# Gated cross-attention block on one core: layer 0's key, value and context preparation on f16 parts, placed in the middle of a step

## What is computed

```python
# layer 0, differential attention: 32 score heads of 4, 16 value heads of 8
k = ctx @ Wk.T ; v = ctx @ Wv.T          # [32, 1500, 128] each
a1 = softmax(q1 @ k1.T / 2) @ v ; a2 = softmax(q2 @ k2.T / 2) @ v
attn = a1 - lam * a2                      # then RMS norm per head, Wp, bp
# layer 1, masked attention: 16 heads of 8, bias on q, k and v
k = ctx @ Wk.T + bk ; v = ctx @ Wv.T + bv
attn = softmax(where(mask, -inf, q @ k.T / sqrt(8))) @ v
x = x + tanh(g) * attention ; x = x + tanh(g) * experts
```

## Time and profile before

| | |
|---|---|
| median of 3 executions | 2541.89 us |
| the profiled execution | 2538.51 us |
| its span | 2536.7 us |
| PE / DVE / ACT / POOL busy | 93% / 66% / 58% / 42% |
| mean granted TensorE clock | 0.952 |

### The profile page before, as it was taken

How to read it: one execution, slowest core, us unless ns; L and a number is a source line. 1 busy time by engine, 2 the same in 40 slices (tenths; PEclk the granted TensorE clock), 3 DMA queues, 4 the chain that set the end, 5 groups by cost and what they waited for, 6 DMA issues and landing times. The chain is left out here.

```text
span 2536.7 us, 64926 instructions
## 1 busy us (share of the span) xinstructions
PE 2371.0 (93%) x26296; PEld 1320.2 (52%) x26296; DVE 1679.8 (66%) x3732; ACT 1471.6 (58%) x2101; POOL 1057.8 (42%) x1150
## 2 busy tenths in 40 slices
PE   4799999999999999999996976999999999999798
PEld 3244444444444444444444763566655666666576
DVE  2587777777777777777782553666666666666444
ACT  2156666666666666666675432566656666666422
POOL 4213323333333333332323347456655565663232
PEclk8589999999999999999997996899999999999799
DMA  3533434534434345343321006567665766753100
GB/s 101 104 72 76 96 95 74 112 78 91 103 78 100 91 78 109 77 96 96 74 43 49 22 28 141 107 127 135 131 121 119 123 133 126 135 130 51 51 1 14
DMA packets 157410, 227.67 MB, mean 90 GB/s; under 512 B 46052, under 2 KB 106596, under 8 KB 156612
## 3 DMA queue, kind: packets, MB, share of 16 engines
q1 hardware_dynamic: 157124, 223.67, 42.4%
HBM read 146.77 MB, written 76.48 MB: 88 GB/s over the span
## 5 line engine op out<-in xcount | busy, mean ns | idle before, releaser
L943 ACT ACTIVATE probs<-score_ps 125x896 f32<-125x896 f32 x1152 | 1011.4, 916 | 159.5 <-PE score_ps L850 158.6
L1001 DVE TENSOR_REDUCE max_part<-max_ps 112x1 f32<-112x500 f32 x1022 | 654.6, 670 | 177.0 <-PE spare_ps L829 87.6
L866 PE MATMUL acc_ps<-probs,vext 125*32 125x224 f32 (+1 forms) x12288 | 675.2, 315 | 3.4 <-issue 2.5
L829 PE MATMUL max_ps<-kstack,qstack 48*112 48x500 f16 x1533 | 522.1, 403 | 6.7 <-DVE max_part L1001 3.4
L1001 DVE TENSOR_REDUCE max_part<-spare_ps 112x1 f32<-112x500 f32 x514 | 344.2, 670 | 148.1 <-PE max_ps L829 147.1
L998 DVE CUSTOM_DVE_ANT_0 kstack<-max_ps,kstack 112x500 f32<-112x500 f32 x511 | 335.2, 675 | 160.2 <-PE max_ps L829 87.8
L720 POOL CAST khl<-kstack 128x500 f16<-128x500 f32 x192 | 115.0, 599 | 700.2 <-ACT kstack L926 510.2
L866 PEld LDWEIGHTS acc_ps<-probs,vext 125*32 125x32 f32 x12288 | 258.1, 108 | 262.2 <-issue 248.7
L850 PE MATMUL score_ps<-qstack,kstack 50*125 50x224 f16 (+1 forms) x6144 | 387.7, 243 | 3.3 <-ACT probs L943 1.9
L850 PEld LDWEIGHTS score_ps<-qstack,kstack 50*125 50x125 f16 x6144 | 304.5, 134 | 136.7 <-issue 95.1
L829 PE MATMUL spare_ps<-kstack,qstack 48*112 48x500 f16 x771 | 310.8, 403 | 7.0 <-DVE max_part L1001 1.9
(11 more groups left out here) (184 smaller groups left out, 2613.3 us busy)
## 6 DMA issues: line engine op xcount, KB each, us to landing
kstack<-k_parts SPq DMA_DIRECT2D x384, 187.5 KB, 6.6
k_parts<-khl SPq DMA_DIRECT2D x128, 375.0 KB, 5.5
ctx_f<-in_ctx SPq DMA_DIRECT2D x32, 750.0 KB
context_parts<-ctx_f SPq DMA_DIRECT2D x32, 750.0 KB, 4.7
ctx_f<-context_parts SPq DMA_DIRECT2D x32, 750.0 KB, 4.3
mask_in<-in_mask SPq DMA_DIRECT2D x128, 82.0 KB
qrows<-q_parts SPq DMA_DIRECT2D x384, 7.0 KB, 7.4
qstack<-max_rows SPq DMA_DIRECT2D x384, 0.9 KB
```

The source lines that it names most:

```text
L829: nc.tensor.matmul(room(("P", n, p))[0:PIECE, 0:TK], qstack[n % SLOTS][rows, c, PIECE * i:PIECE * (i + 1)], kstack[n % SLOTS][rows, c, TK ...
L866: last = nc.tensor.matmul(acc_ps[32 * j:32 * j + 32, TT * S * i:TT * S * (i + 1)].rearrange("p (s c) -> p s c", s=S), vext[n % SLOTS][:, t ...
L943: nc.scalar.activation(probs[t % 2][:, 896 * h:896 * h + 896].rearrange("k (b c) -> k b c", b=2), score_ps[(t * H + h) % 2][0:KT, :, 0:448 ...
L1001: nc.vector.reduce_max(best, scores, AX.X).then_inc(s_red, 1)
```

## The change

Both weights of both layers are scaled by 64 and split once, in the set-up, into an f16 high part and an f16 rest (`w_parts`). The context is split the same way. A projection is then three f16 matmuls into one accumulator (high by high, rest by high, high by rest). In layer 0, ACT copies the turned context as f32 into `context_f`, GpSimd makes the two parts from it in the loop (`split_context`), and DVE does so for the first three entries; there are now two buffers of parts. DRAM holds the parts, of the same size as before, and layer 1 reads them.

The side numbers of `where` get new meanings: 1 is between the two halves of the weighing, ahead of the second search, and 2 is behind the weighing. Layer 0's users are reordered, one for each step, on side 1 (A on side 2). Layer 1's stay behind the weighing; M moves there from its place behind the first search.

```diff
+                    for w in range(2):
+                        weight = small[f"W{'kv'[w]}T{i}"][:, :]
+                        high, low = w_parts[:, i, w, 0, :], w_parts[:, i, w, 1, :]
+                        link(nc.vector.tensor_scalar(weight, weight, QK_UP, None, ALU.mult))
...
+                        link(nc.vector.tensor_copy(high, weight))
+                        link(nc.vector.tensor_tensor(low, weight, high, ALU.subtract))
...
     if L is L0:
-        where = {("V", 0): (0, 1), ("F", 0): (1, 1), ("F", 1): (2, 1), ("V", 1): (3, 1), ("T", 0): (4, 1), ("V", 2): (5, 1),
-                 ("K", 0): (6, 1), ("M", 0): (7, 0), ("T", 1): (7, 1), ("K", 1): (8, 1), ("T", 2): (9, 1), ("K", 2): (10, 1),
-                 ("A", 0): (11, 1)}
-        keyed = [("T", 0), ("K", 0), ("T", 1), ("K", 1), ("T", 2), ("K", 2)]
+        where = {("T", 0): (0, 1), ("F", 0): (1, 1), ("T", 1): (2, 1), ("F", 1): (3, 1), ("T", 2): (4, 1), ("K", 0): (5, 1),
+                 ("V", 0): (6, 1), ("M", 0): (7, 1), ("K", 1): (8, 1), ("V", 1): (9, 1), ("K", 2): (10, 1), ("V", 2): (11, 1),
+                 ("A", 0): (11, 2)}
+        keyed = [(kind, i) for kind in "TK" for i in range(NTHIRD)]
...
             def store_context(n):
-                sp.wait_ge(s_ctxT, NTHIRD * (n + 1))
+                sp.wait_ge(s_cp, low_part(n, LAST_THIRD))
...
+            def split_context(n, i):
+                k = slice(TK * i, TK * i + TK)
+                pool.wait_ge(s_ctxT, NTHIRD * n + i + 1)
...
+                nc.gpsimd.tensor_copy(ctxT[n % 2][:, 0, k], context_f[:, k]).then_inc(s_cp, 1)
+                pool.wait_ge(s_cp, high_part(n, i))
+                nc.gpsimd.tensor_tensor(ctxT[n % 2][:, 1, k], context_f[:, k], ctxT[n % 2][:, 0, k], ALU.subtract).then_inc(s_cp, 1)
...
+                if L is L0 and n + 3 < B:
+                    split_context(n + 3, 0)
+                    split_context(n + 3, 1)
                 if n:
                     finish(n)
+                if L is L0 and n + 3 < B:
+                    split_context(n + 3, 2)
                 if n + 3 < B:
                     split_keys(n + 3)
...
-                    nc.tensor.matmul(spare_ps[:, 0:TK], Wk[:, :], ctxT[n % len(ctxT)][:, TK * i:TK * i + TK],
-                                     start=True, stop=True).then_inc(s_ready, 1)
+                    for k, (w, x) in enumerate(((0, 0), (1, 0), (0, 1))):
+                        last = nc.tensor.matmul(spare_ps[:, 0:TK], Wk[w], ctxT[n % 2][:, x, TK * i:TK * i + TK],
+                                                start=k == 0, stop=k == 2)
...
                     search(searched(n, t, 0))
-                    for user in at_step(n, t, 0):
-                        use(user)
                     for i in range(2):
...
                         if i == 0:
+                            for user in at_step(n, t, 1):
+                                use(user)
                             search(searched(n, t, 1))
-                    for user in at_step(n, t, 1):
+                    for user in at_step(n, t, 2):
                         use(user)
...
-            for user in first_preps:
-                drain(user)
+            for n in range(3 if L is L0 else 0):
+                for i in range(NTHIRD):
+                    k = slice(TK * i, TK * i + TK)
+                    dve.wait_ge(s_ctxT, NTHIRD * n + i + 1)
...
+                    nc.vector.tensor_copy(ctxT[n % 2][:, 0, k], context_f[:, k]).then_inc(s_cp, 1)
+                    dve.wait_ge(s_cp, high_part(n, i))
+                    nc.vector.tensor_tensor(ctxT[n % 2][:, 1, k], context_f[:, k], ctxT[n % 2][:, 0, k], ALU.subtract).then_inc(s_cp, 1)
```

More of the change, by code:

```diff
@@ L268, in carve, with context_parts @@
     return flat.rearrange("p (a b c) -> p a b c", a=shape[0], b=shape[1])
+def context_parts(T, i):
+    return T["ctx_f"][:, i, 0:SK].bitcast(F16).rearrange("p (a k) -> p a k", a=2)
 def load_context(sp, T, L, n):
@@ L274, in load_context @@
     if L.masked:
-        sp.dma_start(T["ctx_f"][:, n % 2, 0:SK], T["ctx_dram"][n:n + 1, :, :].rearrange("b d k -> (b d) k")).then_inc(loaded[n % 2], 16)
+        sp.dma_start(context_parts(T, n % 2), T["ctx_dram"][n:n + 1, :, :, :].rearrange("b d a k -> (b d) a k")).then_inc(loaded[n % 2], 16)
     else:
@@ L463, in attend @@
     ctx_in = ctx_f[0:KT, 1, :].rearrange("p (t d) -> p t d", t=NKT)
-    ctxT = [ctx_f[:, i, 0:SK] for i in range(1 + L.masked)]
     qrows, mask_in, out_sb = T["qrows"], T["mask_in"], T["out_sb"]
@@ L476, in attend @@
     key_f = T["kstack"][1][:, K_WORDS + SK:K_WORDS + 3 * SK].bitcast(F32)
+    ctxT = [context_parts(T, 0), context_parts(T, 1) if L.masked else
+            T["kstack"][2][:, K_WORDS:K_WORDS + 2 * SK].rearrange("p (a k) -> p a k", a=2)]
+    context_f = T["kstack"][0][:, K_WORDS:K_WORDS + 2 * SK].bitcast(F32)
     qstack = [T["qstack"][i][:, 0:PAIRS * GC].rearrange("p (c q) -> p c q", c=PAIRS) for i in range(SLOTS)]
-    Wk, Wv = (small["WkT1"] if L.masked else T["wk_order"]), small[f"WvT{layer}"]
+    Wk, Wv = ([T["w_parts"][:, layer, w, part, :] for part in range(2)] for w in range(2))
     S = L.heads // VH
@@ L558, in attend @@
         for t in range(NKT):
-            order += searched(n, t, 0) + at_step(n, t, 0) + searched(n, t, 1) + at_step(n, t, 1)
+            order += searched(n, t, 0) + at_step(n, t, 1) + searched(n, t, 1) + at_step(n, t, 2)
     order += [(kind, B - 1, i) for kind, i in turnaround]
@@ L802, in use @@
                         c = TK * i + KT * t
-                        last = nc.tensor.matmul(spare_ps[0:KT, D * t:D * t + D], ctxT[n % len(ctxT)][:, c:c + KT], Wv[:, :],
-                                                start=True, stop=True)
+                        for k, (x, w) in enumerate(((0, 0), (0, 1), (1, 0))):
+                            last = nc.tensor.matmul(spare_ps[0:KT, D * t:D * t + D], ctxT[n % 2][:, x, c:c + KT], Wv[w],
+                                                    start=k == 0, stop=k == 2)
                     last.then_inc(s_ready, 1)
@@ L929, in drain @@
                         vext[n % SLOTS][:, THIRD * i:THIRD * i + THIRD, :, :].rearrange("k t u (a e) -> k t (u a) e", a=2)[:, :, :, 0:VD],
-                        spare_ps[0:KT, :].rearrange("k (t h d) -> k t h d", t=THIRD, d=VD), ACT.Copy).then_inc(s_v, 1)
+                        spare_ps[0:KT, :].rearrange("k (t h d) -> k t h d", t=THIRD, d=VD), ACT.Copy,
+                        scale=1.0 / QK_UP).then_inc(s_v, 1)
                 if kind == "F":
@@ L957, in _ @@
                         copy_output(n)
-                    for user in at_step(n, t, 0) + at_step(n, t, 1):
+                    for user in at_step(n, t, 1) + at_step(n, t, 2):
                         drain(user)
```

51 lines of the change are left out of this document (31 added, 20 removed).

## The result

The changed kernel takes **2666.2 us** (median of 4 executions, 2640.2 to 2668.6) beside 2540.5 of the kernel before on the same chip: a ratio of **1.047** (95% interval 1.044 to 1.050), slower by 4.7%. The forecast was 2593, with a range from 2510 to 2635.

What follows compares the result with a forecast made beforehand. PE was taken to bound the kernel, except some 0.3 us a step waiting for DVE. Terms 2.3 - 8 + 91 - 3 - 31 = +51 on 2538.5 gave 2589.8; the median stands 3.4 higher, so 2593, range 2510 to 2635.

Steps and rivals of the forecast that it cites:

- The clock's term: Layer 0's loop, behind T(0)'s wait: TensorE's clock halves and adds 1.2 us to the period, between nothing and 2.0.
- the ring: Layer 0's loop: T(0) to step 7 (20.3), then fill_m, context load and landing (21.0) set a period of 41.3 us.
- the wait: Layer 0, T(0) in step 0: PE waits 4.0 us for the context load in every iteration.
- The second search holds a step at 3.0: Layer 0's steps: the second search's second piece waits for its bank, so no step is under 3.0 us.
- the rival that denied it: Second search not held by its bank: T and F steps of 2.65, period 39.5, total 2509; chance 0.10.
- Step 1 grows by 0.8: Layer 0: step 1's first search piece waits for T(0)'s bank, read out behind the output's copy; step 1 becomes 3.8 us.
- K and V: f16 projections: K takes 0.83 us for 1.03, V 0.90 for 1.07.
- GpSimd's splits for nothing: GpSimd's six operations on the context, 5.0 us more an iteration, cost nothing in total time.
- Layer 1: Layer 1's faster V and K save 1.0 us an iteration, -31 us in all (-20 to -35).
- Ahead of the loop: Before layer 0's loop: set-up adds 2.3 us, the new order of T and K saves 8 (4 to 11).
- The clock stays: Rival: the wait at T(0) comes but the clock stays full; period 41.3, total 2559; chance 0.22.
- The load lands in time: Rival: the context load lands within 8.9 us of issue, no wait; period 37.3, total 2445; chance 0.11.

Runs made afterwards that it cites:

- filled_wait: Changed kernel with 18 f16 matmuls of 500 columns, result unused, ahead of T(0)'s wait for the context in layer 0's loop: 2560.6 us.
- experiment 7: ScalarE reads T(0) out ahead of the output's copy in layer 0's step 0: 2415.4 us against load_at_once's 2440.0; in f32, 2495.0 against 2509.0.
- Experiment 3: The run load_first: changed kernel with layer 0's context store and load ahead of fill_m in SP's list, 2597.8 us.
- load_first: Changed kernel with layer 0's context store and load put ahead of fill_m instead of behind it in SP's list: 2597.8 us, ratio 1.023.
- load_at_once: Changed kernel with layer 0's context load issued once its buffer is free (behind step 4), ahead of the parts' store and fill_m: 2440.0 us, ratio 0.959.
- filled_after: Changed kernel with nine f16 matmuls of 500 columns, result unused, behind T(0)'s wait and ahead of its transposes: 2660.5 us, ratio 1.047.

## Why the prediction was wrong, by its own steps

- **The clock's term failed.** "The rest of step 0, 1.4 long, becomes 2.4, and part of step 1 hides behind T's read-out. I add 1.2, between nothing and 2.0." The first half is right (2.50). The second is not. Of the low clock behind the rest of step 0 the term leaves 0.2, as if the stretch ended in step 1 and T's read-out hid the rest. But the stretch lasts 10.2 to 17.1 us from its start (6.8 once). All of step 1 goes at half clock and takes 5.20 for 3.84, and so does a part of what follows: step 2 takes 3.28 in the stretch shown above, which is 10.2 long, and steps 2 and 3 take 4.79 and 4.02 in the one of 17.1 that begins at 896.3. filled_wait prices it: **3.8 an iteration, not 1.2**. 28 x 2.6 = 73 us is the distance from 2593 to 2666. The bound of 2.0 was worse than the value: no row behind it shows how such a stretch ends, and the range went with it.
- **The other terms nearly cancel.** Beside the clock's 73 stand +4.5 for the ring (28 x 0.16), +1.9 ahead of the loop and some 6 more in layer 0 that I can't give to a term, and against them -9.7 for layer 1. That the clock's term alone makes up the distance is luck to that extent.
- **The direction, the wait and its size were right.** 4.04 for 4.0; the load issued 8.24 behind step 7 for 8.1; 12.59 to T (12.6 to 13.5 over the loop) for 12.9; ordinary steps 3.02 for 3.0, step 7 3.23 for 3.2. The ring of 41.3 is filled_wait's 41.46.
- **The second search holds a step at 3.0**: right. T and F steps are 3.02, not 2.65, and the rival that denied it is out. In the step that begins at 643.05, with F, the second piece goes at S+2.16 (forecast S+2.15), and its weights wait for DVE:

```profile
645.21 0.41 PE L871 MATMUL spare_ps<-kstack,qstack 48*112 48x500 f16 x1
645.21 0.12 PEld L871 LDWEIGHTS spare_ps<-kstack,qstack 48*112 48x112 f16 x1 [0.23 <-DVE max_part L1043]
```

- **Step 1 grows by 0.8**: right, by experiment 7: 3.85, and 3.02 with ScalarE's order turned. In the changed kernel itself it is 5.20, at half clock.
- **K and V** were over-priced by 0.09 and 0.06. A step with K in layer 0 is 3.02, one with V too (3.1 forecast), since the bank holds both.
- **GpSimd's splits for nothing**: right for the loss. Experiment 3 shows the point at which they matter. In the changed kernel the third of them ends 3.0 behind the start of step 7 (658.15 for 655.14), so a store placed ahead of fill_m waits for it, and drags the load along.
- **Layer 1**: forecast 1.0 an iteration. The undisturbed periods went from 23.9 to 22.3, by 1.6; on average it is 1.23 (-33.1 in 27), since seven periods before and nine after are longer, some with a low clock and some without, and those after by more. Why, I did not look for. Steps with V went down by 0.23 each, with K by 0.2 to 0.3. The last K kept its gain, which I had down as lost to fill_m: the step with it went from 2.66 to 2.44. With the stretches on both sides of the loop (-2.0, and -5.6 with the experts and the end) it is -40.7. Forecast were -31, and at most -35.
- **Ahead of the loop** -3.8 for -5.7; the loads of the first entries, sooner, took longer (13.4 and 15.5 to T, 12.6 and 13.1 before).
- **The rivals.** "The clock stays" is what filled_wait made by force; its 2559 met 2560.6. Its argument that a gap must be long is out: in load_first, waits of 2.3 on average (longest 3.2) have a low clock behind them. "The load lands in time" took another list of SP's to come true (load_at_once); its 2445 met 2440.0, with a period of 37.43 for 37.3. Both use the terms above that cancel, so the mechanisms are shown, and the nearness of the totals is in part luck.

The Trainium skill ("TensorE: Matmul & The Clock Gate", section "A second HAM failure mode: psum-queue depth-cycling") tells of a kernel in which short idle times of TensorE between groups of matmuls make the clock go back and forth between its two levels. Whether that is what keeps the clock low here, no run shows: from 632.07 to 640.3 the trace lists one idle time of PE, 0.20 us in step 1. filled_after's nine matmuls have none. What the runs do show is that the work behind the wait matters; the f32 weighing and the small operands are other ways to read it.

What stays open: which property of the steps keeps the clock low, why some low stretches last 10.2 and others 17.1 us in the same code, and what lengthens the disturbed periods of layer 1.

## What to carry to other kernels

A wait of the bounding engine in every turn of a loop costs more than its length when it drops TensorE's clock: here 4.04 of waiting cost 3.8 more. How long the clock stays low depended on the work behind the wait, so price it from a stretch that shows the clock coming back in the kernel's own steps, or by filling the wait. When a consumer is moved to the front of an iteration, move the issue of its load to the point where the buffer is free, and look at what stands next behind it in the same queue: here it had to be ahead of the small DMAs by several us (9.2 and 9.8 did), not by one entry. What the change had in it was worth 4.9%; SP's order made a loss of 4.7% of it, and ScalarE's kept back the last 25 us.

## What the runs showed of the hardware that was not expected

- The low clock outlasts the wait: 10.2 to 17.1 us (one of 6.8) at waits of 4.0, and 3.4 to 17.1 at waits of 2.3 on average (load_first), though the windows have TensorE busy nearly throughout behind the wait. With nine dense matmuls behind the wait it is 3.4 or 6.8.
- 3.8 us of added dense work an iteration, at half clock, cost nothing: 2660.5 beside 2666.2, with the same ratio to the kernel before (1.047).
- Eight DMAs of 0.9 KB took 12.71 us to issue right behind the issue of a load of 750 KB in pieces of 512 B, 5.41 at 9.8 us behind it (load_at_once), 4.89 at 9.2 us behind it with f32 parts, and 4.91 ahead of it.
- Twelve f16 matmuls of 128 columns, each with its own load of weights, start 0.058 apart at full clock; 128 columns at 2.4 GHz are 0.053, so the loads of weights are nearly hidden. The search behind them starts 0.84 after the first.
